# Value matmuls in four short blocks a group, output matmuls in two bunches, in a two-layer attention and experts kernel

## The chip, the cores and the metric

The kernel runs on one core of a Trainium2 chip. The metric is the device time of one execution in microseconds, median of three runs. The engines work side by side, each through its own queue in order: TensorE (PE; its weight loads are shown apart, as PEld), VectorE (DVE), ScalarE (ACT), GpSimd (POOL), and SyncE (SP), which issues the DMAs. They wait for each other by semaphores.

## The reference

There are 8 sequences of 1024 tokens of width 128, and two layers. Each layer adds attention and experts, both of the normalised input, to its input:

```python
xn = layernorm(x);  x = x + attention0(xn) + experts0(xn)
xn = layernorm(x);  x = x + attention1(xn) + experts1(xn)
```

Attention of layer 0, which the change touches, is latent attention with 8 heads. Keys and values come from a latent of 32 columns, and the output goes through W_O:

```python
scores = einsum('bhsd,bhtd->bhst', q, k) * scale      # 1024 x 1024 a head
attn = softmax(scores)
o = einsum('bhst,bhtd->bhsd', attn, v)                # v = latent @ W_UV + b
return o.transpose(...) @ W_O + b_O
```

Experts of layer 0: 8 experts, silu(x @ gate) * (x @ up) @ down, two experts a token by weight. Layer 1 has a linear attention and 8 other experts.

## The kernel before

One loop runs over the 8 sequences. The queries' heads come in two quads of four heads. A tile t is one head and one block of 128 queries; 64 tiles make 16 groups, a group g being the four heads of a quad for one block of queries (n = g % 8). Every engine has a function attention_step(w), and the steps w = 0 to 71 have, in each quad, four steps for the query projections (L1266) and 32 steps with one tile each. Which work of an older tile or group stands in step w is set by lags counted from the tile or the last tile of the group. The step of tile t is t + 4 in the first quad and t + 8 in the second.

In step w PE does the scores of tile t (L1213, 6 matmuls of 64*128 weights into two of four PSUM banks 0 to 3, after the exp of two steps before), then the 16 transposes of the probabilities of the tile of step w - 2 (L1232, into banks 4 and 5, after both copies of the tile before it), then what stands in this step of the groups. DVE takes the maximum of the scores (L863), copies the upper half of the transposed tile to probsT (L871), and in the steps 8 to 38 does one small operation of the router of the experts. ACT copies the lower half (L587) and does exp with the sum of the row (L599). probsT has room for two groups, so the copies wait for u_ready of the group two before.

The work of a group, with its lag behind the last tile's step, is this:

- lag 1: DVE takes the reciprocal of the row sums (L881)
- lags 3 and 5: PE's values(g, i), i = 0 and 1, each 16 matmuls (4 key blocks by 4 heads, 32 loads of 128*32 in the trace, L1247) that add up in the columns 0 to 127 of bank 6 + g % 2; behind i = 1 come 4 matmuls (8 loads, L1254) that spread the reciprocals in the columns 128 to 255, and u_ready
- lag 7: ACT copies these to scale_sb (L612)
- lag 8: DVE multiplies, to o_latent (L887), two slots
- lag 9: PE's output(g), one matmul (2 loads, L1261) with the quad's half of W_O, to the columns 256 to 383 of the bank
- lag 10: DVE adds them to block n of x_mid (L895); o_added lets values(g + 2, 0) start

In numbers of steps: values stand in even steps only, and output in every fourth, together with values(i = 1). After step 73 the experts of layer 0 begin (function experts, gate and up L1151, 32 units, down L1158), and PE, ACT and DVE call attention_step(74 + u) within unit u, which finishes the last groups. The gates' transposes and copy (L1129, L546) stand in step 39 and 40. The second layer does not use these steps.

The instructions of an engine run in program order, so the order of the calls is the schedule. SP loads the expert weights and the gate rows; none of its orders is written in attention_step.

Of the kernel before, what the change touches and what calls it, by code (L numbers as in the profile page):

```python
# [9 lines left out]
ALU = mybir.AluOpType  # L10
# [3 lines left out]
P = 128  # L14
BATCH = 8
SEQ = 1024
NT = SEQ // P
D = 128
BANK = 512
# [10 lines left out]
QUADS = H0 // QUAD  # L30
# [11 lines left out]
OUTPUT_LAG = 9  # L42
ADDED_LAG = 10
# [97 lines left out]
def two_layer_kernel(nc, ins, out):  # L141
    with ExitStack() as ctx:  # L142
# [26 lines left out]
        out_room = sb("out_room", [P, 2, 2, P])  # L169
        scale_sb, o_latent = out_room[:, 0, :, :], out_room[:, 1, :, :]  # L170
# [51 lines left out]
        ffn_u = [ffn_u2[:, 0, :], ffn_u2[:, 1, :], out_room[:, :, :, :].rearrange("p a b c -> p (a b c)")]  # L222
# [100 lines left out]
        o_ready = signal("o_ready", GROUPS)  # L323
        o_added = signal("o_added", GROUPS)
# [340 lines left out]
        def _(dve):  # L665
# [75 lines left out]
            for index in range(BATCH):  # L741
# [110 lines left out]
                def attention_step(w):  # L852
# [30 lines left out]
                    if g is not None:  # L883
                        if g >= 2:
                            dve.wait_ge(o_ready.sem, o_ready.at(b, g - 1))
                        dve.wait_ge(scale_ready.sem, scale_ready.at(b, g + 1))
                        nc.vector.tensor_tensor(o_latent[:, g % 2, :], ps[:, 6 + g % 2, 0:P],  # L887
                                                scale_sb[:, g % 2, :], ALU.mult).then_inc(u_scaled.sem, 1)
                    g = group_at(w, ADDED_LAG)
                    if g is not None:  # L890
                        n = g % NT
                        if g >= NT:
                            dve.wait_ge(o_added.sem, o_added.at(b, g - NT + 1))
                        dve.wait_ge(o_ready.sem, o_ready.at(b, g + 1))
                        nc.vector.tensor_tensor(x_mid[:, n, :], x_mid[:, n, :],  # L895
                                                ps[:, 6 + g % 2, 2 * P:3 * P], ALU.add
                                                ).then_inc(o_added.sem, 1)
# [46 lines left out]
                dve.wait_ge(o_added.sem, o_added.at(b, GROUPS))  # L944
# [131 lines left out]
        def _(pe):  # L1076
# [126 lines left out]
            for index in range(BATCH):  # L1203
# [33 lines left out]
                def values(g, i):  # L1237

                    if i == 0:
                        pe.wait_ge(low_copied.sem, low_copied.at(b, (g + 1) * QUAD))  # L1240
                        pe.wait_ge(high_copied.sem, high_copied.at(b, (g + 1) * QUAD))
                        if g >= 2:

                            pe.wait_ge(o_added.sem, o_added.at(b, g - 1))
                    for k in range(4 * i, 4 * i + 4):
                        for j in range(QUAD):
                            nc.tensor.matmul(ps[DC * j:DC * (j + 1), 6 + g % 2, 0:P], latent[:, k, :],  # L1247
                                             probsT[:, (g % 2) * QUAD + j, k * P:(k + 1) * P],
                                             start=(k == 0), stop=(k == NT - 1))
                    if i == 1:  # L1250
# [8 lines left out]
                def output(g):  # L1259
                    pe.wait_ge(u_scaled.sem, u_scaled.at(b, g + 1))  # L1260
                    nc.tensor.matmul(ps[:, 6 + g % 2, 2 * P:3 * P], o_latent[:, g % 2, :], w_o[:, g // NT, :],  # L1261
                                     start=True, stop=True).then_inc(o_ready.sem, 1)
# [7 lines left out]
                def attention_step(w):  # L1270
# [30 lines left out]
                    g = group_at(w, OUTPUT_LAG)  # L1301
                    if g is not None:
                        output(g)
                    for i in range(2):
                        g = group_at(w, VALUES_LAG + 2 * i)
                        if g is not None:
                            values(g, i)
# [152 lines left out]
```

## Time and profile before

| | us |
|---|---|
| median of 3 runs | 3281.0 |
| lowest and highest | 3280.36, 3284.69 |
| the profiled execution | 3290.3 |
| its span, first to last instruction | 3288.4 |
| PE busy | 2786.6 (85%) |
| DVE busy | 2251.3 (68%) |
| ACT busy | 1494.3 (45%) |
| POOL busy | 761.5 (23%) |
| mean granted TensorE clock | 0.954 |

The profile is of one execution, so its durations are summed against its own 3290.3 us. Busy shares are means over eight sequences of about 401 us, each with an attention stretch of about 180 us (steps 0 to 73) and the experts of two layers. A PE that is busy in the table may still wait inside a chain, since the ends of matmuls are modelled.

### The profile page before, as it was taken

How to read it: one execution, taken by the hardware profiler on the slowest of the kernel's cores; microseconds unless marked ns; L12 is line 12 of the kernel's file. 1: busy time of each engine (PE TensorE's matmuls, PEld its weight loads, DVE VectorE, ACT ScalarE, POOL GpSimd, SP SyncE). 2: the span in 40 equal slices, each digit the busy share in tenths (PEclk: the TensorE clock that was granted, in tenths of full speed). 3: DMA queues.
4: the chain of work that ended last, by engine and by line, in shares of the span. 5: the costliest groups of instructions: out<-in, count | busy, mean ns of one | idle time of the engine just before them, and what ended most of it. 6: DMA issues, size and time to landing. Idle time of an engine off the chain costs nothing. (4 is left out here: it accounts for less than half of the span.)

```text
span 3288.4 us, 66221 instructions
## 1 busy us (share of the span) xinstructions
PE 2786.6 (85%) x26912; PEld 1928.6 (59%) x26912; DVE 2251.3 (68%) x3638; ACT 1494.3 (45%) x2489; POOL 761.5 (23%) x566
## 2 busy tenths in 40 slices
PE   4889798897888988889888888888888888988978
PEld 2656456665556655565555655556565565655655
DVE  3874678747776478764877648775487755977558
ACT  2763237622466224662246523565135652266422
POOL 0004230052300533004320144101351023500325
PEclk7999899998999989999999999999899998999989
DMA  5002110022100221002210012000120012200112
GB/s 219 8 28 71 65 52 8 28 77 71 40 8 28 77 74 42 22 15 71 87 30 28 20 59 90 27 28 31 48 93 24 28 39 72 69 17 28 59 56 74
DMA packets 81734, 165.34 MB, mean 50 GB/s; under 512 B 8271, under 2 KB 26904, under 8 KB 80920
## 3 DMA queue, kind: packets, MB, share of 16 engines
q1 hardware_dynamic: 81432, 161.11, 14.9%
q8 instruction: 214, 3.51, 0.4%
q14 instruction: 88, 0.72, 0.1%
HBM read 147.97 MB, written 13.11 MB: 49 GB/s over the span
## 5 line engine op out<-in xcount | busy, mean ns | idle before, releaser
L498 POOL TENSOR_TENSOR probs<-ffn_gu,gate_bc 128x512 f32<-128x512 f32 x416 | 558.6, 1344 | 2268.4 <-DVE ffn_gu L925 1748.2
L1151 PE MATMUL ps<-x_parts,w_split 128*128 128x512 f32 x3072 | 941.5, 443 | 82.4 <-DVE ffn_u L964 41.7
L1151 PEld LDWEIGHTS ps<-x_parts,w_split 128*128 128x128 f32 x3072 | 570.0, 190 | 384.7 <-issue 161.3
L863 DVE TENSOR_REDUCE neg_max<-ps 128x1 f32<-128x1024 f32 x512 | 624.2, 1220 | 225.5 <-PE ps L1213 209.1
L599 ACT ACTIVATE probs<-ps,neg_max 128x1024 f32<-128x1024 f32 x512 | 571.7, 1117 | 138.4 <-DVE neg_max L863 135.0
L1232 PEld LDWEIGHTS ps<-ident,probs 64*128 64x128 f32 x8192 | 327.3, 141 | 354.9 <-issue 328.4
L1232 PE MATMUL ps<-ident,probs 64*128 64x64 f32 x8192 | 360.7, 228 | 201.3 <-DVE probsT L871 200.7
L1213 PE MATMUL ps<-keys,q_parts 64*128 64x512 f32 x3072 | 499.4, 431 | 35.2 <-ACT probs L599 21.2
L1158 PE MATMUL ps<-probs,w_down 128*128 128x512 f32 x832 | 431.1, 604 | 42.7 <-POOL probs L498 41.9
L587 ACT COPY probsT<-ps 128x512 f32<-128x512 f32 x512 | 300.5, 587 | 257.6 <-PE ps L1232 256.2
L925 DVE TENSOR_TENSOR ffn_gu<-ffn_s,ps 128x512 f32<-128x512 f32 x256 | 176.1, 688 | 332.8 <-ACT ffn_s L624 330.4
L641 ACT ACTIVATE ffn_s<-ffn_g 128x512 f32<-128x512 f32 x256 | 159.9, 631 | 459.9 <-DVE ffn_g L960 459.1
L871 DVE COPY probsT<-ps 128x512 f32<-128x512 f32 x512 | 348.8, 681 | 21.9 <-PE ps L1232 21.7
L624 ACT ACTIVATE ffn_s<-ps 128x512 f32<-128x512 f32 x256 | 153.0, 598 | 419.2 <-PE ps L1151 419.2
L1213 PEld LDWEIGHTS ps<-keys,q_parts 64*128 64x128 f32 x3072 | 256.7, 190 | 123.6 <-issue 44.8
L1247 PE MATMUL ps<-probsT,latent 128*32 128x128 f32 x8192 | 280.1, 278 | 16.1 <-DVE x_mid L895 16.1
L1247 PEld LDWEIGHTS ps<-probsT,latent 128*32 128x32 f32 x8192 | 210.0, 110 | 48.7 <-issue 26.2
L1158 PEld LDWEIGHTS ps<-probs,w_down 128*128 128x128 f32 x832 | 156.9, 191 | 108.8 <-POOL probs L498 64.5
L960 DVE TENSOR_SCALAR ffn_g<-ps,b_gate 128x512 f32<-128x512 f32 x256 | 190.8, 745 | 15.4 <-PE ps L1151 11.5
L856 DVE SCALAR_TENSOR_TENSOR q_parts<-ps,b_q,q_parts 128x1024 fp32r<-128x1024 f32 x64 | 82.1, 1283 | 119.0 <-ACT q_parts L570 119.0
L1066 DVE SCALAR_TENSOR_TENSOR ffn_gu<-ffn_u,ffn_s 128x512 f32<-128x512 f32 x176 | 134.3, 767 | 37.8 <-ACT ffn_s L641 31.8
L498 POOL TENSOR_TENSOR ffn_h<-ffn_gu,gate_bc 128x512 f32<-128x512 f32 x96 | 123.6, 1288 | 140.2 <-DVE ffn_gu L1066 95.0
(170 smaller groups left out, 2518.3 us busy)
## 6 DMA issues: line engine op xcount, KB each, us to landing
w_split<-w_parts SPq DMA_DIRECT2D x260, 256.0 KB, 2.6
gate_bc<-gate_rows SPq DMA_DIRECT2D x128, 512.0 KB, 4.2
w_parts<-q_parts SPq DMA_DIRECT2D x4, 2048.0 KB, 9.1
x_in<-in_x SPq DMA_DIRECT2D x9, 512.0 KB, 4.2
out<-x_mid SPq DMA_DIRECT2D x8, 512.0 KB, 3.2
probsT<-in_gate_up SPq DMA_DIRECT2D x1, 2048.0 KB, 8.7
gate_bc<-in_gate_up SPq DMA_DIRECT2D x1, 2048.0 KB, 13.0
w_down<-in_down SPq DMA_DIRECT2D x2, 1024.0 KB
```

The source lines that it names most:

```text
L498: nc.gpsimd.tensor_tensor(ffn_h[u % 5], ffn_gu[:, u % 3, :], gate_bc[:, e % GATE_SLOTS, c * BANK:(c + 1) * BANK], ALU.mult).then_inc(h_rea ...
L587: nc.scalar.copy(half_of(t, 0), half_turned(0)).then_inc(low_copied.sem, 1)
L599: nc.scalar.activation(probs[:, t % 3, :], banks(2 * (t % 2)), ACT.Exp, bias=neg_max[:, t % 4:t % 4 + 1], accum_out=row_sum[:, g % 2, t % ...
L863: nc.vector.tensor_reduce(neg_max[:, t % 4:t % 4 + 1], banks(2 * (t % 2)), X, ALU.max, negate=True).then_inc(max_ready.sem, 1)
L871: nc.vector.tensor_copy(half_of(t, 1), half_turned(1)).then_inc(high_copied.sem, 1)
L925: nc.vector.tensor_tensor(ffn_gu[:, u % 3, :], ffn_s[:, u % 3, :], ps[:, 2 + u % 2, :], ALU.mult).then_inc(gu_done.sem, 1)
L960: nc.vector.tensor_scalar(ffn_g[:, u % 3, :], ps[:, u % 2, :], b_gate[:, f:f + 1], LIMIT, ALU.add, ALU.min).then_inc(gate_lim.sem, 1)
L1151: mm = nc.tensor.matmul(ps[:, bank, :], w_split[:, f % 4, h, k * P:(k + 1) * P], tokens[:, half], start=(part == 0), stop=(part == 2))
L1158: nc.tensor.matmul(ps[:, 4 + c, :], w_down[l][:, f, :], ffn_h[u % 5], start=(l == 0 and f == 0), stop=(f == E * FH - 1)).then_inc(down_don ...
L1213: mm = nc.tensor.matmul(ps[:, 2 * (t % 2) + c, :], q_parts[rows, j, q, n * P:(n + 1) * P], keys[rows, k, :], start=(part == 0), stop=(part ...
L1232: mm = nc.tensor.transpose(ps[:, 4 + c, k * HQ:(k + 1) * HQ], probs[rows, t % 3, k * P:(k + 1) * P], ident[rows, rows])
L1247: nc.tensor.matmul(ps[DC * j:DC * (j + 1), 6 + g % 2, 0:P], latent[:, k, :], probsT[:, (g % 2) * QUAD + j, k * P:(k + 1) * P], start=(k == ...
```

## The change

The value matmuls of a group, before in two calls of four key blocks (lags 3 and 5), stand in four calls of two key blocks (lags 3, 4, 5, 6); the scale matmuls stay behind the last. The output matmuls of the 16 groups leave steps of their own: they run in two bunches, in steps 78 and 80 (units 4 and 6 of the first experts), each 8 matmuls for four blocks of queries, the two quads added up in PSUM, into a whole bank (6 and 7). o_latent has a slot for each group. DVE adds each bunch with one operation of 128x512 one step later, in place of 16 of 128x128. values(g, 0) waits for u_scaled of group g - 2 in place of o_added, and the multiplication L887 waits no more for o_ready.

```diff
--- before.py
+++ after.py
@@ -39,8 +39,7 @@
 VALUES_LAG = 3
 SCALES_LAG = 7
 SCALED_LAG = 8
-OUTPUT_LAG = 9
-ADDED_LAG = 10
+OUTPUT_STEPS = (STEPS + 6, STEPS + 8)
 ROUTER_STEP = 8
 ROUTER_EXP_STEPS = (18, 20)
 SPLIT_STEP = 30
@@ -166,8 +165,9 @@
         neg_max = sb("neg_max", [P, 4])
         row_sum = sb("row_sum", [P, 2, QUAD])
         inv_sum = sb("inv_sum", [P, 2, QUAD])
-        out_room = sb("out_room", [P, 2, 2, P])
-        scale_sb, o_latent = out_room[:, 0, :, :], out_room[:, 1, :, :]
+        out_room = sb("out_room", [P, BANK])
+        scale_sb = out_room[:, 0:2 * P].rearrange("p (a b) -> p a b", a=2)
+        o_latent = sb("o_latent", [P, QUADS, NT, P])
 
 
 
@@ -219,7 +219,7 @@
         ffn_s = sb("ffn_s", [P, 3, BANK])
         ffn_g, ffn_u2 = sb("ffn_g", [P, 3, BANK]), sb("ffn_u2", [P, 2, BANK])
 
-        ffn_u = [ffn_u2[:, 0, :], ffn_u2[:, 1, :], out_room[:, :, :, :].rearrange("p a b c -> p (a b c)")]
+        ffn_u = [ffn_u2[:, 0, :], ffn_u2[:, 1, :], out_room[:, :]]
         ffn_h4 = sb("ffn_h4", [P, BANK])
         ffn_gu = sb("ffn_gu", [P, 3, BANK])
 
@@ -320,8 +320,8 @@
         u_ready = signal("u_ready", GROUPS)
         scale_ready = signal("scale_ready", GROUPS)
         u_scaled = signal("u_scaled", GROUPS)
-        o_ready = signal("o_ready", GROUPS)
-        o_added = signal("o_added", GROUPS)
+        o_ready = signal("o_ready", 2)
+        o_added = signal("o_added", 2)
         x_high_ready = signal("x_high_ready", 2)
         x_low_ready = signal("x_low_ready", 2)
         raw_in = [signal(f"raw_in{l}") for l in range(2)]
@@ -881,19 +881,14 @@
                         nc.vector.reciprocal(inv_sum[:, g % 2, :], row_sum[:, g % 2, :]).then_inc(inv_ready.sem, 1)
                     g = group_at(w, SCALED_LAG)
                     if g is not None:
-                        if g >= 2:
-                            dve.wait_ge(o_ready.sem, o_ready.at(b, g - 1))
                         dve.wait_ge(scale_ready.sem, scale_ready.at(b, g + 1))
-                        nc.vector.tensor_tensor(o_latent[:, g % 2, :], ps[:, 6 + g % 2, 0:P],
+                        nc.vector.tensor_tensor(o_latent[:, g // NT, g % NT, :], ps[:, 6 + g % 2, 0:P],
                                                 scale_sb[:, g % 2, :], ALU.mult).then_inc(u_scaled.sem, 1)
-                    g = group_at(w, ADDED_LAG)
-                    if g is not None:
-                        n = g % NT
-                        if g >= NT:
-                            dve.wait_ge(o_added.sem, o_added.at(b, g - NT + 1))
-                        dve.wait_ge(o_ready.sem, o_ready.at(b, g + 1))
-                        nc.vector.tensor_tensor(x_mid[:, n, :], x_mid[:, n, :],
-                                                ps[:, 6 + g % 2, 2 * P:3 * P], ALU.add
+                    if w - 1 in OUTPUT_STEPS:
+                        c = OUTPUT_STEPS.index(w - 1)
+                        dve.wait_ge(o_ready.sem, o_ready.at(b, c + 1))
+                        nc.vector.tensor_tensor(x_mid[:, 4 * c:4 * c + 4, :], x_mid[:, 4 * c:4 * c + 4, :],
+                                                ps[:, 6 + c, :].rearrange("p (n d) -> p n d", d=D), ALU.add
                                                 ).then_inc(o_added.sem, 1)
 
                 for w in range(UNIT_STEP):
@@ -941,7 +936,7 @@
                         if k == 0:
                             dve.wait_ge(rstd_ready.sem, rstd_ready.at(b, 1))
                         norm_apply(0, x_in, (2 * k, 2 * k + 1))
-                dve.wait_ge(o_added.sem, o_added.at(b, GROUPS))
+                dve.wait_ge(o_added.sem, o_added.at(b, 2))
                 experts_add(0)
 
                 for c in range(2):
@@ -1241,13 +1236,13 @@
                         pe.wait_ge(high_copied.sem, high_copied.at(b, (g + 1) * QUAD))
                         if g >= 2:
 
-                            pe.wait_ge(o_added.sem, o_added.at(b, g - 1))
-                    for k in range(4 * i, 4 * i + 4):
+                            pe.wait_ge(u_scaled.sem, u_scaled.at(b, g - 1))
+                    for k in range(2 * i, 2 * i + 2):
                         for j in range(QUAD):
                             nc.tensor.matmul(ps[DC * j:DC * (j + 1), 6 + g % 2, 0:P], latent[:, k, :],
                                              probsT[:, (g % 2) * QUAD + j, k * P:(k + 1) * P],
                                              start=(k == 0), stop=(k == NT - 1))
-                    if i == 1:
+                    if i == NT // 2 - 1:
 
                         pe.wait_ge(inv_ready.sem, inv_ready.at(b, g + 1))
                         for j in range(QUAD):
@@ -1256,10 +1251,14 @@
                                                   start=True, stop=True)
                         mm.then_inc(u_ready.sem, 1)
 
-                def output(g):
-                    pe.wait_ge(u_scaled.sem, u_scaled.at(b, g + 1))
-                    nc.tensor.matmul(ps[:, 6 + g % 2, 2 * P:3 * P], o_latent[:, g % 2, :], w_o[:, g // NT, :],
-                                     start=True, stop=True).then_inc(o_ready.sem, 1)
+                def output(c):
+
+                    pe.wait_ge(u_scaled.sem, u_scaled.at(b, GROUPS - 1 + c))
+                    for n in range(4 * c, 4 * c + 4):
+                        for quad in range(QUADS):
+                            mm = nc.tensor.matmul(ps[:, 6 + c, (n % 4) * P:(n % 4 + 1) * P], o_latent[:, quad, n, :],
+                                                  w_o[:, quad, :], start=(quad == 0), stop=(quad == QUADS - 1))
+                    mm.then_inc(o_ready.sem, 1)
 
                 def queries(h):
                     for c in range(HALVES):
@@ -1298,11 +1297,10 @@
                         pe.wait_ge(low_copied.sem, low_copied.at(b, NT * QUAD))
                         pe.wait_ge(high_copied.sem, high_copied.at(b, NT * QUAD))
                         gates_transpose(b, 0)
-                    g = group_at(w, OUTPUT_LAG)
-                    if g is not None:
-                        output(g)
-                    for i in range(2):
-                        g = group_at(w, VALUES_LAG + 2 * i)
+                    if w in OUTPUT_STEPS:
+                        output(OUTPUT_STEPS.index(w))
+                    for i in range(NT // 2):
+                        g = group_at(w, VALUES_LAG + i)
                         if g is not None:
                             values(g, i)
 
```

## Rows read from the trace of the kernel before

**Rows 1.** The page, part 1: busy us (share of the span) xinstructions.
```profile
PE 2786.6 (85%) x26912; PEld 1928.6 (59%) x26912; DVE 2251.3 (68%) x3638; ACT 1494.3 (45%) x2489; POOL 761.5 (23%) x566
```

**Rows 2.** PE's longest wait: us in total, times, longest us.
```profile
PE ps L1232 <- DVE probsT L871: 200.7, 245, 2.3
```

**Rows 3.** Windows: us, busy (x) of PE, PEld, DVE, ACT, POOL, then granted clock.
```profile
1426.61:1436.65 10.04, 8.38 (x170) 6.49 (x166) 7.59 (x12) 7.19 (x13) 0.00 (x0) 1.00 0.01 2
...
1321.75:1331.80 10.05, 8.35 (x166) 6.45 (x162) 8.29 (x16) 7.47 (x15) 0.00 (x0) 1.00 0.01 2
...
1371.00:1389.00 18.00, 14.91 (x166) 8.01 (x164) 7.85 (x10) 6.76 (x10) 0.00 (x0) 0.91 0.01 2
```

**Rows 4.** Timeline, steps 58 to 62: start us, us, engine, line, operation [idle before].
```profile
1429.22 0.81 PEld L1247 LDWEIGHTS ps<-probsT,latent 128*32 128x32 f32 x32
...
1430.24 0.97 PE L1213 MATMUL ps<-keys,q_parts 64*128 64x512 f32 x6
...
1431.31 1.22 DVE L863 TENSOR_REDUCE neg_max<-ps 128x1 f32<-128x1024 f32 x1 [0.95 <-PE ps L1213]
...
1432.45 0.68 DVE L871 COPY probsT<-ps 128x512 f32<-128x512 f32 x1
1432.63 1.11 ACT L599 ACTIVATE probs<-ps,neg_max 128x1024 f32<-128x1024 f32 x1 [0.26 <-DVE neg_max L863]
1433.05 0.28 DVE L887 TENSOR_TENSOR out_room<-ps,out_room 128x128 f32<-128x128 f32 x1
1433.25 1.22 DVE L863 TENSOR_REDUCE neg_max<-ps 128x1 f32<-128x1024 f32 x1
...
1433.28 0.71 PE L1232 MATMUL ps<-ident,probs 64*128 64x64 f32 x16 [0.82 <-DVE probsT L871]
...
1433.92 0.30 PEld L1261 LDWEIGHTS ps<-w_o,out_room 128*128 128x128 f32 x2
...
1434.34 0.81 PEld L1247 LDWEIGHTS ps<-probsT,latent 128*32 128x32 f32 x32
...
1435.13 0.24 PEld L1254 LDWEIGHTS ps<-ident,inv_sum 128*32 128x32 f32 x8
...
1435.57 0.53 PEld L1213 LDWEIGHTS ps<-keys,q_parts 64*128 64x128 f32 x6 [0.20 <-issue]
...
1436.81 0.54 PEld L1213 LDWEIGHTS ps<-keys,q_parts 64*128 64x128 f32 x6
```

**Rows 5.** Timeline: PE at steps 16 and 36 of one sequence.
```profile
1317.79 0.53 PEld L1213 LDWEIGHTS ps<-keys,q_parts 64*128 64x128 f32 x6
...
1368.12 1.98 PE L1266 MATMUL ps<-xT,w_q 128*128 128x512 f32 x4
```

**Rows 6.** Timeline: PE at steps 45 and 73.
```profile
1395.88 0.53 PEld L1213 LDWEIGHTS ps<-keys,q_parts 64*128 64x128 f32 x6
...
1465.64 0.58 PEld L1232 LDWEIGHTS ps<-ident,probs 64*128 64x128 f32 x16 [0.20 <-issue]
```

**Rows 7.** Timeline: the border of the two quads, steps 38, 39 and 41.
```profile
1378.11 0.68 DVE L871 COPY probsT<-ps 128x512 f32<-128x512 f32 x1
...
1379.13 1.08 PE L1247 MATMUL ps<-probsT,latent 128*32 128x128 f32 x32 [2.01 <-DVE x_mid L895]
...
1380.14 3.61 PE L1266 MATMUL ps<-xT,w_q 128*128 128x512 f32 x4
...
1389.21 1.22 DVE L863 TENSOR_REDUCE neg_max<-ps 128x1 f32<-128x1024 f32 x1 [1.66 <-PE ps L1213]
```

**Rows 8.** Timeline of PE's weight loads in the experts of both layers.
```profile
1473.23 0.30 PEld L1261 LDWEIGHTS ps<-w_o,out_room 128*128 128x128 f32 x2 [0.67 <-DVE out_room L887]
...
1656.62 0.42 PEld L1158 LDWEIGHTS ps<-probs,w_down 128*128 128x128 f32 x2
...
1658.87 0.43 PEld L1158 LDWEIGHTS ps<-ffn_h,w_down 128*128 128x128 f32 x2
...
1662.91 0.43 PEld L1158 LDWEIGHTS ps<-probs,w_down 128*128 128x128 f32 x2
```

## The prediction

> **What bounds the kernel now.** I read the busy shares first [rows 1]: PE is busy 85% of the span, but in the attention it is not full, and its largest wait is that of the transposes L1232 for the DVE copy L871, 245 times and 200.7 us together [rows 2]. Then windows of four steps (one group) in either quad: 10.03 to 10.05 us each, PE not at its rate, DVE busy 7.59 us in the second quad and 8.29 us in the first, where the router's small operations stand on it, ACT 7.19 and 7.47 [rows 3]. No engine fills the 10.04 us, so a chain through several engines sets them.
>
> The timeline shows it [rows 4]. Scores of step 59 start at 1430.24; the maximum L863 starts 1.07 later (1431.31), the copy L871 1.14 after that (1432.45), the transposes of step 60 0.83 after that (1433.28): 3.04 in all. Then PE needs 0.64 for these 16 transposes, and does the work that stands behind them in step 60 before the scores of step 61 can start. So the scores of step n+2 come no earlier than 3.68 + v(n+1) after those of step n, v being PE's value, scale and output work of step n+1. The scores and transposes between, of the odd step and the scores of the even one (1435.57 to 1436.81: 1.24 for a step without group work), fit below the DVE part. There are two such chains, of odd and of even steps. Today all of v stands in even steps: 1.01 for 16 value matmuls (1429.22 to 1430.23), and 0.42 + 0.79 + 0.44 = 1.65 for output, values and scale (1433.92, 1434.34, 1435.13, 1435.57). The chain of odd scores carries both: 2 x 3.68 + 1.01 + 1.65 = 10.02, and the window says 10.03. The other chain carries nothing (7.36) and waits.
>
> **The change, part by part.** *Value matmuls in four steps.* A block of 32 loads takes 0.81 and the scores start 0.20 behind it; behind the scale matmuls there is again 0.20 [rows 4]. So a block of 16 takes, by halving the 0.81 and keeping the 0.20, 0.605. If all of it halves it is 0.505; if nothing does, 1.01. I take 0.605, as the 0.20 is the same behind a block of 32 and behind one of 8. The last block has 8 scale loads besides: 0.825. Both chains now carry two blocks: the heavier 0.605 + 0.825, so a group takes 7.36 + 1.43 = 8.79. The lighter takes 8.57 and is held by the other. Saved: 1.24 a group (1.28 in the first quad, where 1317.79 to 1368.12 are five groups of 10.07 [rows 5]).
>
> The rows show these 0.20 on the way out of a block; on the way in, behind the transposes, there is none that I can see (rival 2). A rule of the Trainium skill speaks against the change here: by TensorEngine Tiling, section Tiling Modes (Key Properties), changing the tiling mode drains the array, and two more value blocks (128*32) amid scores and transposes (64*128) make four more such changes a group. By that rule it is rival 2 that holds, 3207; by the rows the sum below.
>
> *What else must keep up at 8.79.* PE's issue work is 4 x 1.24 + 3 x 0.605 + 0.825 = 7.6. DVE's in the first quad is 8.29 less the one L895 of 0.28 = 8.0, some 8.3 with its gaps: close, but under. ACT has 7.5. Exp starts 1.32 after the maximum (1432.63) and is done before the chain gets to the scores two steps on. u_ready comes one step later (lag 6, not 5). The copies L587/L871 into the same slots of probsT, one step after it, wait for transposes that PE issues behind that block anyway; behind them on DVE stands the next maximum. So nothing is late there. The scale copy stays at lag 7.
>
> *Output matmuls and L895 leave the attention.* Each costs 0.42 in v; it is in the 1.65 already. L895, 0.20 net on DVE (as L887: 1433.05 to 1433.25), lies under the chain and is worth nothing but room. The values now wait for u_scaled, an operation that is older by two steps.
>
> *Sum for one sequence.* (a) Steps 16 to 36: 5 x 1.28 = 6.4, less about 0.64, because the chain that ends in step 36 is the even one and begins behind a value block that step 15 did not have: 5.76. (b) The border of the quads. The values of step 38 wait for L895 2.01 us, but the copy L871 that they need as well ends at 1378.79, 0.34 before they start [rows 7], so that 0.2 of it can go; with half of the values moved on, the queries at 1380.14 start 0.6 earlier. In step 40 the output and its wait no longer stand ahead of the scores of 41, whose maximum waited 1.66; the copy of the gates on ACT takes back half: 0.8. Output of step 44: 0.42. Together 1.8. (c) Steps 45 to 73, 1395.88 to 1465.64 [rows 6]: 6.5 groups x 1.24 = 8.06, and 0.65 at the end, where step 72 has no output and half the values: 8.7. (d) First experts, where PE is the limit: leave 1.01 (step 74), 1.65 and a wait of 0.67 (step 76, [rows 8]), 0.42 (step 80) = 3.75. Come 3 x 0.605 + 0.825 = 2.64 for group 15, and two bunches of 8 matmuls = 16 loads each. Nearest row: the 16 loads of the same shape of the projection stretch one unit from 2.25 (1656.62 to 1658.87) to 4.04 (to 1662.91) [rows 8], so 1.79 each, 3.58. Net +2.47. The two additions of four blocks (128x512) lie on DVE in units where it waits for PE's 2.25 us units.
> Sum: 5.76 + 1.8 + 8.7 - 2.47 = 13.8 us, eight times 110. No DMA and no SP or POOL instruction is moved.
> The profiled execution took 3290.3 (span 3288.4), 9.3 above the median of 3281.0. 3290.3 - 110 = 3180; the median scaled alike 3281 - 110 = 3171.
>
> **The clock.** At the border of the quads, behind the wait of 2.01 us, the queries take 3.61 [rows 7] where the same four took 1.98 [rows 5]: that stretch ran at 1.2 GHz, the one before at 2.4, and the window around it has a mean granted clock of 0.91 [rows 3]. The wait shrinks to about 1; if the clock then stays up, 1.6 us more are won, 13 in eight sequences. I leave it as it is in the sum, and put it in the range.
>
> **Rivals.**
> 1. *All small costs fall away:* blocks of 0.505 (0.2 more a group, 11.5 groups: 2.3), clock up at the border (1.6), the lighter chain sets the last step (1.0): 13.8 + 4.9 = 18.7 a sequence, 3131. For it: nothing but the shortness of the blocks; against: the 0.20 stands behind every one. Chance 0.13.
> 2. *A short block pays on its way in too.* With another 0.20 for each of the two blocks of a chain the period is 9.19, 11.5 x 0.40 = 4.6 us of gain go in a sequence: 9.2 left, 3207. For it: a block amid transposes and scores is a change of shape on both sides. Against: in rows 4 the values' loads start 0.12 behind the output's and close behind the transposes. Chance 0.10.
> 3. *Short blocks cost as much as long ones, or DVE becomes the bound in the first quad.* With 1.01 a block: 7.36 + 1.01 + 1.23 = 9.60, so only 0.43 a group; 11.5 x 0.81 = 9.3 less gain, 0.8 more in the experts: 3.7 a sequence, 3252. With DVE bound at 9.4 in the first quad: 5 x 0.6 = 3 less, 3195; both in part: 3215 to 3250. Chance 0.10.
> 4. *Nothing of the period is won:* another wait takes it, say the maximum held behind DVE's own queue at 10.03. Left are 1.8 + 0.65 - 2.47, that is 0: 3281. The DVE sum of 7.6 in the second quad speaks against it. Chance 0.03.
> 5. *Slower:* u_ready a step later does hold the copies of the group after next, and with them maximum, exp and scores behind them. If each group lost a whole step of 2.2, 25.3 would go in a sequence: 11.5 slower, 3373. It decides from 1.2 us a group on. Against it: the copy waits for transposes issued behind the block. Chance 0.04.
> Forecast as summed, with small deviations either way (3145 to 3200): 0.60.
>
> **How the numbers follow.** A measurement tells 0.2% (6.6 us) from no change. The forecast and rivals 1 to 3 are faster: 0.93; rival 4 is the same, 0.03; rival 5 slower, 0.04. Range: 3135 takes in most of rival 1, 3215 rival 2 and the DVE bound; outside are the rest of rival 3, rivals 4 and 5 and the end of 1, less than 0.2.
>
> **What the profile after should show.** Value loads in blocks of 16, each followed by 0.20; four-step windows of 8.8 us (8.6 to 9.0) in both quads, nearly even steps of 2.2; L1232's wait for L871 far below 200 us but not gone, in pieces of 0.3; DVE's share up to 70% or more; the output line with 256 loads as before, in bunches of 16 that stretch two units by 1.8. Wrong would be: windows of 9.2 or 9.6 (the block cost), windows of 10 (another wait), L871 waiting with PE's L1254 as releaser (rival 5), or long stretches at 1.2 GHz inside the quads.

## The result and the profile after

The changed kernel takes 3170.25 us (median of 4 runs, 3162.18 to 3171.23), the kernel before on the same chip 3282.85 (4 runs, 3280.36 to 3288.09). The ratio is 0.965, 95% interval 0.9629 to 0.967: 3.5% faster, where 3171 was forecast. The profiled execution took 3170.15, its span is 3168.1, against 3288.4 before.

The page of the changed kernel, part 1:

```profile
PE 2811.7 (89%) x26912; PEld 1902.6 (60%) x26912; DVE 2245.2 (71%) x3526; ACT 1494.5 (47%) x2489; POOL 760.9 (24%) x566
```

PE has as many instructions as before, and its share has gone from 85% to 89% [rows 1]: the span is 120 us shorter because PE waits less. The view of PE's waits in the changed kernel says which; its columns are us in total, times, and the longest:

```profile
PE ps L1227 <- DVE probsT L871: 62.1, 103, 2.0
```

The transposes (L1227 now, L1232 before) wait 62.1 us for the copy L871 in place of 200.7, and 103 times in place of 245 [rows 2]; that is 0.6 a time, where the prediction looked for pieces of 0.3. Two windows of one group (four steps) each, columns as in [rows 3]:

```profile
1376.50:1385.27 8.77, 8.54 (x165) 6.18 (x162) 7.57 (x11) 7.23 (x14) 0.00 (x0) 1.00 0.02 5
1385.27:1394.02 8.75, 8.51 (x164) 6.16 (x161) 7.57 (x11) 7.23 (x14) 0.00 (x0) 1.00 0.01 2
```

A group takes 8.75, and took 10.04. DVE's and ACT's work in it is what it was; it is packed closer. The timeline of the second of these groups (start, length, engine, operation, idle before):

```profile
1385.27 0.53 PEld L1208 LDWEIGHTS ps<-keys,q_parts 64*128 64x128 f32 x6 [0.20 <-issue]
...
1386.67 0.38 PEld L1242 LDWEIGHTS ps<-probsT,latent 128*32 128x32 f32 x16
...
1387.24 0.53 PEld L1208 LDWEIGHTS ps<-keys,q_parts 64*128 64x128 f32 x6 [0.20 <-issue]
...
1388.32 0.71 PE L1227 MATMUL ps<-ident,probs 64*128 64x64 f32 x16
...
1388.96 0.38 PEld L1242 LDWEIGHTS ps<-probsT,latent 128*32 128x32 f32 x16
...
1389.54 0.53 PEld L1208 LDWEIGHTS ps<-keys,q_parts 64*128 64x128 f32 x6 [0.20 <-issue]
...
1391.50 0.53 PEld L1208 LDWEIGHTS ps<-keys,q_parts 64*128 64x128 f32 x6 [0.20 <-issue]
...
1393.22 0.38 PEld L1242 LDWEIGHTS ps<-probsT,latent 128*32 128x32 f32 x16
...
1393.58 0.24 PEld L1249 LDWEIGHTS ps<-ident,inv_sum 128*32 128x32 f32 x8
...
1394.02 0.53 PEld L1208 LDWEIGHTS ps<-keys,q_parts 64*128 64x128 f32 x6 [0.20 <-issue]
```

Every step holds a block of 16 value loads now, and the scores of the next step start 0.58 after the block does (1388.96 to 1389.54: 0.38 and 0.20); with the scale loads it is 0.80 (1393.22 to 1394.02). One group of the heavier chain: 1385.27 to 1389.54 is 4.27 (3.68 + 0.58 = 4.26), and 1389.54 to 1394.02 is 4.48 = 3.68 + 0.80. Sum 8.75.

Where the time of one sequence goes, from starts in the two traces (means over the eight sequences; the quad stretches between the 12th and 32nd, the 32nd and 38th, and the 38th and last maximum L863; the experts from the 1st to the 32nd multiplication L920):

| stretch | before | after | difference |
|---|---|---|---|
| first maximum to step 15 | 26.2 | 25.7 | -0.5 |
| steps 15 to 35 (first quad) | 50.3 | 45.0 | -5.3 |
| steps 35 to 45 (border of the quads) | 29.1 | 26.6 | -2.5 |
| steps 45 to 71 (second quad) | 64.5 | 56.5 | -8.1 |
| to the first L920 of the experts | 9.2 | 7.7 | -1.5 |
| first experts, units 0 to 31 | 70.0 | 73.2 | +3.2 |
| rest of the experts, into the next sequence | 153.1 | 152.6 | -0.5 |

The sum is -15.3 a sequence, 122 in eight (the last row counts seven times), and the spans differ by 120.3.

The border: PE's operations there in the changed kernel, from the timeline.

```profile
1326.11 0.64 PE L1242 MATMUL ps<-probsT,latent 128*32 128x128 f32 x16 [0.97 <-issue]
...
1326.69 1.98 PE L1265 MATMUL ps<-xT,w_q 128*128 128x512 f32 x4
```

The wait ahead of the values is 0.97 in place of 2.01, and the queries behind it take 1.98 in place of 3.61 [rows 7]: the granted clock stayed at 2.4 GHz where it had gone to 1.2.

The first experts of the changed kernel, PE's loads:

```profile
1403.97 0.38 PEld L1242 LDWEIGHTS ps<-probsT,latent 128*32 128x32 f32 x16 [0.36 <-issue]
1404.55 1.22 PEld L1146 LDWEIGHTS ps<-x_parts,w_split 128*128 128x128 f32 x6 [0.20 <-issue]
...
1412.51 0.42 PEld L1153 LDWEIGHTS ps<-probs,w_down 128*128 128x128 f32 x2
...
1413.60 1.75 PEld L1259 LDWEIGHTS ps<-w_o,o_latent 128*128 128x128 f32 x15 [0.24 <-issue]
...
1416.55 0.43 PEld L1153 LDWEIGHTS ps<-probs,w_down 128*128 128x128 f32 x2
...
1418.81 0.42 PEld L1153 LDWEIGHTS ps<-probs,w_down 128*128 128x128 f32 x2
```

A unit with a bunch of output matmuls takes 4.04 (1412.51 to 1416.55), the next without one 2.26: 1.78 for a bunch, 1.79 was forecast. The value blocks among the gate matmuls are another matter. The weight loads stand idle for 0.36 ahead of such a block and for 0.20 behind it. What a block costs in all shows in the distance from one unit's multiplication L920 on DVE to the next one's. In the changed kernel, a unit with a short block:

```profile
1404.71 0.69 DVE L920 TENSOR_TENSOR ffn_gu<-ffn_s,ps 128x512 f32<-128x512 f32 x1 [2.51 <-ACT ffn_s L624]
1406.88 0.69 DVE L920 TENSOR_TENSOR ffn_gu<-ffn_s,ps 128x512 f32<-128x512 f32 x1 [1.48 <-ACT ffn_s L624]
```

In g1_last_two, an experiment below that has long blocks there, a unit with a long block, one without a block, and one with a long block and the scale:

```profile
1405.26 0.69 DVE L920 TENSOR_TENSOR ffn_gu<-ffn_s,ps 128x512 f32<-128x512 f32 x1 [2.51 <-ACT ffn_s L624]
1407.86 0.69 DVE L920 TENSOR_TENSOR ffn_gu<-ffn_s,ps 128x512 f32<-128x512 f32 x1 [1.91 <-ACT ffn_s L624]
1409.22 0.69 DVE L920 TENSOR_TENSOR ffn_gu<-ffn_s,ps 128x512 f32<-128x512 f32 x1 [0.47 <-ACT ffn_s L624]
1412.04 0.69 DVE L920 TENSOR_TENSOR ffn_gu<-ffn_s,ps 128x512 f32<-128x512 f32 x1 [2.13 <-ACT ffn_s L624]
```

That is 2.17 with a short block, 2.60 with a long one, 1.36 without, 2.82 with a long one and the scale. A short block adds about 0.80 there and a long one 1.24, where the prediction had 0.605 and 1.01.

### The profile page after: what moved, and what is told of

It is laid out like the page before. It is cut to its first block and busy times, and to the rows that moved or that the text cites. A ratio compares the mean times of both kernels' runs of the same rounds, so it can differ in the third digit from the quotient of the medians.

```text
span 3168.1 us, 65933 instructions
## 1 busy us (share of the span) xinstructions
PE 2811.7 (89%) x26912; PEld 1902.6 (60%) x26912; DVE 2245.2 (71%) x3526; ACT 1494.5 (47%) x2489; POOL 760.9 (24%) x566
## 3 DMA queue, kind: packets, MB, share of 16 engines
q1 hardware_dynamic: 81432, 161.11, 15.3%
## 5 line engine op out<-in xcount | busy, mean ns | idle before, releaser
L863 DVE TENSOR_REDUCE neg_max<-ps 128x1 f32<-128x1024 f32 x512 | 624.5, 1221 | 113.8 <-PE ps L1208 78.8
L1227 PEld LDWEIGHTS ps<-ident,probs 64*128 64x128 f32 x8192 | 323.9, 141 | 246.4 <-issue 228.1
L1227 PE MATMUL ps<-ident,probs 64*128 64x64 f32 x8192 | 362.0, 228 | 81.8 <-DVE probsT L871 62.1
L920 DVE TENSOR_TENSOR ffn_gu<-ffn_s,ps 128x512 f32<-128x512 f32 x256 | 175.9, 687 | 350.1 <-ACT ffn_s L624 347.6
L871 DVE COPY probsT<-ps 128x512 f32<-128x512 f32 x512 | 348.2, 680 | 13.2 <-PE ps L1227 13.2
L1242 PE MATMUL ps<-probsT,latent 128*32 128x128 f32 x8192 | 331.9, 280 | 7.8 <-issue 7.8
L1242 PEld LDWEIGHTS ps<-probsT,latent 128*32 128x32 f32 x8192 | 193.7, 109 | 64.1 <-issue 33.6
```

What stands on the lines that cost most here:

```text
L863: nc.vector.tensor_reduce(neg_max[:, t % 4:t % 4 + 1], banks(2 * (t % 2)), X, ALU.max, negate=True).then_inc(max_ready.sem, 1)
L871: nc.vector.tensor_copy(half_of(t, 1), half_turned(1)).then_inc(high_copied.sem, 1)
L920: nc.vector.tensor_tensor(ffn_gu[:, u % 3, :], ffn_s[:, u % 3, :], ps[:, 2 + u % 2, :], ALU.mult).then_inc(gu_done.sem, 1)
L1227: mm = nc.tensor.transpose(ps[:, 4 + c, k * HQ:(k + 1) * HQ], probs[rows, t % 3, k * P:(k + 1) * P], ident[rows, rows])
```

## The experiments

The theory is that of the prediction: two chains of steps, scores n+2 = scores n + 3.68 + v(n+1), so what matters is how PE's group work is shared between odd and even steps. Rivals: that the bunches (less work in the quads, fewer waits) bring the gain, or that PE's work in a group as a whole counts, wherever it stands. In the first four, each part alone and two other splits of the values.

### e1_values4: the values in four steps, the outputs as before

```diff
 (kernel before)
-                    for k in range(4 * i, 4 * i + 4):
+                    for k in range(2 * i, 2 * i + 2):
...
-                    if i == 1:
+                    if i == NT // 2 - 1:
...
-                    for i in range(2):
-                        g = group_at(w, VALUES_LAG + 2 * i)
+                    for i in range(NT // 2):
+                        g = group_at(w, VALUES_LAG + i)
```

> The kernel before with the value matmuls in four steps (lags 3 to 6), outputs as before. Theory of the two chains (scores of step n+2 not before 3.68 us + group work of step n+1): even steps carry 0.60 + 0.60 + 0.42 of output, a group takes 8.98 us, eight sequences give some 100 us, and the clock at the border of the quads stays up as in the changed kernel: 3165 to 3185 us. Rival (the gain comes from taking outputs and their additions off the queues): at most half of the 113 us of the whole change, 3225 or more.

Measured: 3172.85 (4 runs, 3166.88 to 3183.30), ratio 0.9672 (0.9649 to 0.9696). Steps 15 to 35 take 45.7, steps 45 to 71 57.7, the first experts 70.1. So the split of the values brings all of the gain. A group takes 8.95 in the second quad, and the sum of the two chains is 8.98. The bunches bring 0.7 and 1.2 more in the quads and 0.8 at their border, and pay 3.1 in the experts: nothing net that can be told at the interval. The profiled executions lie 13 us apart (spans 3181.4 and 3168.1), and that is not the bunches' doing either: 14 us of it are the last row of the table, 154.6 for 152.6, whose code is the same in both.

### e2_bunches: the changed kernel with the values in lags 3 and 5 again

```diff
 (changed kernel)
-                    for k in range(2 * i, 2 * i + 2):
+                    for k in range(4 * i, 4 * i + 4):
...
-                    if i == NT // 2 - 1:
+                    if i == 1:
...
-                    for i in range(NT // 2):
-                        g = group_at(w, VALUES_LAG + i)
+                    for i in range(2):
+                        g = group_at(w, VALUES_LAG + 2 * i)
```

> The changed kernel with the value matmuls in two steps as before (lags 3 and 5), so the bunches alone. Two chains: both blocks in even steps, 7.36 + 1.01 + 1.23 = 9.60 us a group, less 2 us of bunches in the experts: 3235 to 3265 us. Rival (outputs are the cost): 3225 or less.

Measured: 3264.11 (3262.80 to 3265.33), ratio 0.9947 (0.9932 to 0.9962). Starts of the scores in its timeline (PE):

```profile
1420.91 0.96 PE L1208 MATMUL ps<-keys,q_parts 64*128 64x512 f32 x6
1422.17 0.94 PE L1208 MATMUL ps<-keys,q_parts 64*128 64x512 f32 x6
...
1430.52 0.96 PE L1208 MATMUL ps<-keys,q_parts 64*128 64x512 f32 x6
```

A group takes 9.61 (1420.91 to 1430.52): 2 x 3.68 + 1.01 + 1.23 = 9.60. Without the output matmul of 0.42 in the heavy chain a group is 0.42 shorter, and that is all that the bunches do for it.

### e3_lags34: two blocks of 16 matmuls in neighbouring steps (lags 3 and 4)

```diff
 (changed kernel)
-                    for k in range(2 * i, 2 * i + 2):
+                    for k in range(4 * i, 4 * i + 4):
...
-                    if i == NT // 2 - 1:
+                    if i == 1:
...
-                    for i in range(NT // 2):
+                    for i in range(2):
                         g = group_at(w, VALUES_LAG + i)
```

> The changed kernel with the values of a group in two blocks of 16 matmuls, but in neighbouring steps (lags 3 and 4), so one in an even and one in an odd step, and none in the other two. Two chains: each carries one block, the heavier 7.36 + 1.23 = 8.59 us a group, and the experts have two short blocks less: 3145 to 3165 us, below the changed kernel's 3170. Rival (what helps is that every step carries the same, PE having no empty steps): worse than the changed kernel by a good part of the way back, 3200 to 3250.

Measured: 3264.18 (3263.02 to 3268.09), ratio 0.9951 (0.9932 to 0.9969). This missed: each chain carries one block, and yet a group takes 9.10. One group in its timeline:

```profile
1420.22 0.96 PE L1208 MATMUL ps<-keys,q_parts 64*128 64x512 f32 x6
...
1422.84 0.96 PE L1208 MATMUL ps<-keys,q_parts 64*128 64x512 f32 x6
...
1423.91 1.22 DVE L863 TENSOR_REDUCE neg_max<-ps 128x1 f32<-128x1024 f32 x1 [0.60 <-ACT probs L599]
...
1425.05 0.68 DVE L871 COPY probsT<-ps 128x512 f32<-128x512 f32 x1
...
1425.73 1.19 DVE L863 TENSOR_REDUCE neg_max<-ps 128x1 f32<-128x1024 f32 x1
...
1426.84 0.68 DVE L871 COPY probsT<-ps 128x512 f32<-128x512 f32 x1
...
1427.67 0.71 PE L1227 MATMUL ps<-ident,probs 64*128 64x64 f32 x16 [0.20 <-DVE probsT L871]
...
1428.31 0.81 PEld L1242 LDWEIGHTS ps<-probsT,latent 128*32 128x32 f32 x32
...
1429.32 0.54 PEld L1208 LDWEIGHTS ps<-keys,q_parts 64*128 64x128 f32 x6 [0.20 <-issue]
```

The trace shows a third chain, which passes from one step to the next on DVE. Two heavy steps stand in a row: the scores behind the second start 2.62 after those behind the first (1420.22, 1422.84). From there 1.07 to the maximum, 1.14 to its copy L871, and the next maximum follows that copy on DVE at once (0.68); 1.11 to its copy, 0.83 to the transposes, 0.64 to the value block, 1.01 to the scores: 2.62 + 1.07 + 1.14 + 0.68 + 1.11 + 0.83 + 0.64 + 1.01 = 9.10. In the changed kernel the same chain is 1.97 (1385.27 to 1387.24) + 5.47 + 0.58 = 8.02, below the 8.75 of the heavier parity chain, so there it doesn't show. The first quad bears the chain out: there a small router operation stands on DVE between that copy and the next maximum, the maximum starts 0.92 behind the copy and not 0.68, and a group takes 9.37 in place of 9.10. Even parity is not enough; the work has to be even from step to step.

The quads (47.6 in seven of eight sequences, and 59.3, against 45.0 and 56.5) make 5.4 a sequence, 43 of its 94 us. The rest lies mostly outside them: 28.5 for 26.6 at their border, 8.5 for 7.7 behind the second, 155.6 for 152.6 in the last stretch, with a mean granted clock of 0.945 in place of 0.961 over the span.

### e4_1313: the four steps with 1, 3, 1 and 3 key blocks

```diff
 (changed kernel)
-                    for k in range(2 * i, 2 * i + 2):
+                    for k in ((0,), (1, 2, 3), (4,), (5, 6, 7))[i]:
```

> The changed kernel with one, three, one, three key blocks in the four steps. Same work, same number of blocks. Two chains: odd steps carry 0.78 + 1.00, a group takes 9.14 us in place of 8.75: 3198 to 3215 us. Rival (only the total of PE and the number of blocks count): 3165 to 3175.

Measured: 3210.84 (3209.74 to 3217.74), ratio 0.9789 (0.9772 to 0.9807); steps 15 to 35 take 46.7, steps 45 to 71 58.7. Two maxima of its second quad, one group apart (DVE):

```profile
1388.79 1.23 DVE L863 TENSOR_REDUCE neg_max<-ps 128x1 f32<-128x1024 f32 x1
...
1397.98 1.22 DVE L863 TENSOR_REDUCE neg_max<-ps 128x1 f32<-128x1024 f32 x1
```

A group takes 9.19, where the sum of the chain is 9.14. As many matmuls and as many blocks as in the changed kernel, only uneven over the parities: of its gain of 112.6 us, 40.6 are lost. In the profiled executions, which lie 48 us apart, 32 of them stand in the quads and 13 in the last stretch, whose code is the same.

### e5_odd and e6_even: 16 more matmuls a group on the light chain, or on the heavy one

Both add to the kernel before 16 value matmuls a group whose weights are zeros, so that they add nothing to the sums; only the lag at which they stand differs.

```diff
 (kernel before; e6_even has 3 in place of 4)
...
+            nc.vector.memset(zeros[:, :], 0.0)
...
+                    g = group_at(w, 4)
+                    if g is not None and g < GROUPS - 1:
+                        for k in range(4):
+                            for j in range(QUAD):
+                                nc.tensor.matmul(ps[DC * j:DC * (j + 1), 6 + g % 2, 0:P], zeros[:, :],
+                                                 probsT[:, (g % 2) * QUAD + j, k * P:(k + 1) * P],
+                                                 start=False, stop=False)
```

> The kernel before with 16 more matmuls a group (of the form of the values, weights of zeros, so they add nothing) in an odd step (lag 4), where PE has no group work. They take 0.81 + 0.20 us, 15 times a sequence: 121 us of PE in all. Two chains: the chain that they load has 1.66 us of room, so only the block at the border of the quads shows: 0 to +12 us, 3281 to 3295. Rival (PE's total counts): +100 to +120 us, 3380 to 3400.

> The kernel before with the same 16 matmuls more a group in an even step (lag 3), directly behind the values there. Two chains: the full 0.81 us each time, 12 to 15 times a sequence: +78 to +97 us, 3360 to 3380. Rival (PE's total counts): the same as in the odd step.

Measured: e5_odd 3284.39 (10 runs, 3280.95 to 3294.15) beside 3283.44 of the kernel before, ratio 1.0005 (0.9996 to 1.0015). e6_even 3377.85 (3366.48 to 3390.01), ratio 1.0295 (1.0271 to 1.0319). The same 1920 matmuls (16 in 15 groups of 8 sequences) change nothing that can be told on one chain and cost 94 us on the other. A group of the second quad, in e5_odd (PE's loads) and in e6_even (DVE):

```profile
1430.76 0.53 PEld L1215 LDWEIGHTS ps<-keys,q_parts 64*128 64x128 f32 x6 [0.20 <-issue]
...
1440.89 0.53 PEld L1215 LDWEIGHTS ps<-keys,q_parts 64*128 64x128 f32 x6 [0.20 <-issue]
```

```profile
1458.28 1.23 DVE L865 TENSOR_REDUCE neg_max<-ps 128x1 f32<-128x1024 f32 x1 [1.84 <-PE ps L1215]
...
1469.17 1.23 DVE L865 TENSOR_REDUCE neg_max<-ps 128x1 f32<-128x1024 f32 x1 [1.82 <-PE ps L1215]
```

It takes 10.13 and 10.89, and 10.03 in the kernel before: 0.10 on the light chain, 0.86 on the heavy one. The light chain had 2.66 of room (10.02 - 7.36), so the block of 1.01 fits in with 1.65 to spare. This rules out that PE's work in a group as a whole sets the time. That e5_odd comes out at no change at all is partly luck. Its quads take 0.9 a sequence more, and its border 1.0 more where both ran at the full clock (28.5 for 27.5), some 15 us in all; the granted clock gave that back (mean 0.963 over its span, 0.954 in the profiled execution before).

### g1_last_two and g2_values4_last_two: the last group's values in two blocks

What the changed kernel loses in the experts is in part the short blocks of group 15. Here that group alone has two blocks of 16 matmuls; g1_last_two is the changed kernel with it, g2_values4_last_two is e1_values4 with it.

```diff
 (changed kernel)
                 def values(g, i):
+                    if g == GROUPS - 1:
+                        if i % 2:
+                            return
+                        blocks = range(4 * (i // 2), 4 * (i // 2) + 4)
+                    else:
+                        blocks = range(2 * i, 2 * i + 2)
...
-                    for k in range(2 * i, 2 * i + 2):
+                    for k in blocks:
...
-                    if i == NT // 2 - 1:
+                    if blocks[-1] == NT - 1:
```

> The changed kernel, but the values of the last group (15), which run within the first experts, in two blocks of four key blocks (lags 3 and 5) in place of four. If a value block among the experts' matmuls costs 0.36 us on its way in and 0.20 on its way out, two blocks fewer give 1.1 us a sequence: the stretch of the first experts falls from 73.2 to 72.1 us, the time by 9 us to 3161. Rival (PE's gaps there are waits for other engines): no change, 3170.

> Value matmuls in four steps with the outputs as in the kernel before (the first experiment), and the last group in two blocks. The same 1.1 us a sequence below that experiment's 3172.9: 3164. If bunches of outputs are worth something once the values are spread, it is slower than the one before it in this list by that.

Measured: g1_last_two 3181.43 (3178.78 to 3182.40), ratio 0.9685 (0.9664 to 0.9706); g2_values4_last_two 3177.09 (3171.97 to 3179.94), ratio 0.9673 (0.9653 to 0.9692). Both missed. In g1_last_two the first experts are shorter by 0.7 a sequence (72.5 for 73.2), where 1.1 was expected: the four short blocks add 3 x 0.80 + 1.02 = 3.4 and the two long ones 1.24 + 1.46 = 2.7, so not all of the 0.36 ahead of a block is the block's own cost. In g2_values4_last_two they are shorter by only 0.2, since the output matmul of step 76 waits 0.67 for L887 again, as in the kernel before. The time did not follow: in g1_last_two the last stretch, whose code is the same, takes 155.6 to 156.3 in six of seven sequences, where it took 151.5 to 153.6. One case, at the start of the second layer's experts, is the window 1500 to 1515 of g1_last_two (after the busy times stands the mean granted clock):

```profile
1500.00:1515.00 15.00, 10.79 (x33) 7.11 (x32) 8.44 (x17) 0.00 (x0) 0.00 (x0) 0.84 0.00 0
```

and the same window of the changed kernel:

```profile
1500.00:1515.00 15.00, 9.95 (x42) 6.54 (x40) 10.26 (x21) 0.80 (x1) 0.00 (x0) 1.00 0.00 0
```

In the window before (1476 to 1500) both have a mean granted clock of 0.72. PE's gate matmuls behind the same wait, in g1_last_two:

```profile
1506.92 2.65 PE L1146 MATMUL ps<-x_parts,w_split 128*128 128x512 f32 x6 [2.08 <-DVE ffn_g L955]
```

and the changed kernel:

```profile
1506.63 1.62 PE L1146 MATMUL ps<-x_parts,w_split 128*128 128x512 f32 x6 [2.08 <-DVE ffn_g L955]
```

The same wait, the same six matmuls, 0.29 apart in time: in g1_last_two they take 2.65, at a mean granted clock of 0.55, that is mostly at 1.2 GHz; in the changed kernel 1.62, at 2.4 GHz.

### g3_dve_small: one more 128x64 DVE operation in each step of the second quad

The first quad gained less than five groups of 1.28, and I put that down to the router's small operations on DVE. The changed kernel, with one such operation a step in the second quad as well (and from step 40, at the end of the border), on tiles that nobody reads then:

```diff
 (changed kernel)
...
+                        if 40 <= w < 72:
+                            link(nc.vector.tensor_tensor(r_e[:, :, :], r_d[:, :, :], r_d[:, :, :], ALU.add))
```

> The changed kernel with one more small DVE operation (128x64, with its wait, as the router's) behind each copy L871 in the steps of the second quad. If it is these operations that make a group of the first quad 9.0 us and not 8.7, the second quad becomes the same: steps 45 to 71 take 58.5 in place of 56.4 us, and the time rises by 15 to 20 us to 3185 to 3190. Rival (they lie in DVE's idle time, and the first quad is slower for another reason): 3170 to 3174.

Measured: 3182.52 (3181.84 to 3183.13), ratio 0.9689 (0.9665 to 0.9714). The time is near the forecast of the theory and the stretch is not. Steps 45 to 71 take 56.7, 0.3 more: 0.04 a group, so small operations are not it. Of the five groups of the first quad in the changed kernel, four take 8.77 to 8.79 in most sequences and the last 9.77. DVE's timeline there, in the changed kernel:

```profile
1304.34 1.23 DVE L863 TENSOR_REDUCE neg_max<-ps 128x1 f32<-128x1024 f32 x1
...
1306.54 1.21 DVE L849 TENSOR_TENSOR x_parts<-xT,x_parts 128x1024 fp32r<-128x1024 f32 x1
1307.67 1.22 DVE L863 TENSOR_REDUCE neg_max<-ps 128x1 f32<-128x1024 f32 x1
```

One long operation, L849 for the experts' x_parts, stands on DVE between two maxima, and that step takes 3.33 (1304.34 to 1307.67). It takes 3.33 before as well, but there the heavy steps took 3.14 anyway, and its group 10.08. So the 12 us in the time say nothing for the theory: 2 are in the second quad, the rest at the borders (27.1 for 26.6, where these operations stand too, and up to 156.2 in the last stretch).

### h1_pad4 and h2_pad10: more work ahead of the border

If the last stretch of g1_last_two is longer only by where in time the clock's stretches at 1.2 GHz fall, then more work ahead of it can make the kernel faster. g1_last_two, with 4 or 10 repeated matmuls of 128x512 in unit 20 of the first experts (into a bank that is started anew behind them):

```diff
 (g1_last_two; h2_pad10 has 10 in place of 4)
+                    if l == 0 and u == 20:
+                        for i in range(4):
+                            nc.tensor.matmul(ps[:, u % 2, :], w_split[:, f % 4, 0, 0:P], x_high[:, half],
+                                             start=True, stop=True)
```

> The kernel with the last group in two blocks (3181.4 us), with four repeated matmuls of 128x512, about 0.9 us, in unit 20 of the first experts of each sequence. In that kernel 155.9 us pass from the last unit of the first experts to the first maximum of the next sequence, in the changed kernel 151.7 to 153.6, since there PE stays at 2.4 GHz in the first gate and up matmuls of the second layer. Theory: whether it does depends on when in time the border of the layers comes, not on the work; then more work can make the kernel faster or leave it alone: 3155 to 3182 us. Rival (the slow clock belongs to the shorter value blocks' change): 8 x 0.9 us more, 3188 to 3190.

> The same with ten repeated matmuls, about 2.2 us a sequence. Theory: the part after the border shortens by up to 4 us in some or all sequences: 3165 to 3185 us. Rival (work counts as such): 8 x 2.2 us more than 3181.4, 3198 to 3200.

Measured: h1_pad4 3177.85 (3174.0 to 3180.3), ratio 0.967 (0.9653 to 0.9688); h2_pad10 3191.68 (3189.41 to 3194.01), ratio 0.9716 (0.9702 to 0.9731). With four more matmuls the first experts take 73.4, 0.9 more than in g1_last_two, 7 us in all; the last stretch takes 153.6 to 153.9 in five of seven sequences, 2 less, and the median is 3.6 us lower, which the two intervals do not tell apart; what can be told is that the 7 us more of work do not show. With ten, the experts take 74.8, 18 us more in all, and the time is 10.3 longer: outside what I expected of the theory (3165 to 3185) and below what the rival needs (3198 to 3200). That the time of the last stretch shifts with work ahead of it is shown by the stretches of one profiled execution each; a rule by which it could be foretold is not.

## Why the prediction was right, and where its terms were off

*The bound* [rows 2, 4]: right. e5_odd and e6_even show the two chains directly, and the length of a group follows the sum of the heavier chain in four kernels: 8.75 for 8.79 here, 8.95 for 8.98 (e1_values4), 9.61 for 9.60 (e2_bunches), 9.19 for 9.14 (e4_1313). Incomplete in one place: the third chain, over DVE, that e3_lags34 brought out; it doesn't bind in either kernel.

*The block.* 0.605 forecast, 0.58 measured; with the scale 0.825 and 0.80. Period 8.79 and 8.75. In the quads the 0.20 stands on the way out alone, as the rows said.

*(a), steps 16 to 36:* 5.76 forecast, 5.3 measured from step 15 to 35, and 5.4 over the prediction's own stretch. Four groups gained 1.28 each; the fifth, in which L849 sets a step, gained 0.3 (10.08 to 9.77). The 0.64 that was taken off for the first step did not show: L849 took 1.0 instead, which the prediction did not have.

*(b), the border of the quads:* 1.8 forecast, 2.5 measured, but of two parts. In the one sequence of before in which the clock stayed up, this stretch took 27.5; against it the change wins 1.0. The other 1.5 is the clock: the 1.6 that the prediction named and left out of its sum. e1_values4, with the clock up, has 27.4 there: the split values win 0.1 of the 1.0, where the prediction had 0.6 for them, and the outputs the rest.

*(c), steps 45 to 73:* 8.7 forecast; 8.1 to step 71, and 0.7 in the stretch behind it in the sequences of before that ran at the full clock (8.3 or 8.4, and now 7.6 or 7.7). The remaining 0.8 of that row comes from three sequences of before with 10.5 to 11.0, part of them at 1.2 GHz.

*(d), the first experts:* +2.47 forecast, +3.2 measured. The bunches are right at 1.78. The value block was mis-sized there: the prediction took its cost amid scores and transposes, and among 128x512 matmuls it costs more, a short one 0.80 and not 0.605, a long one 1.24 and not 1.01. So the four that come add 3.4, where 2.64 was reckoned. What leaves is 3.6, not 3.75: 1.24 in unit 0, 2.20 in unit 2 with the output and its wait, and 0.20, not 0.42, for the output matmul of step 80 (that unit took 2.46, its neighbours 2.26). With the bunches' 3.56 that gives +3.3, and the sequences of before that the clock left alone have +3.3.

The Trainium skill (TensorEngine Tiling, section Tiling Modes, Key Properties) says that a change of tiling mode drains the array. The traces agree in the idle time of 0.20 of the weight loads behind every value block. Ahead of a block they show 0.36 behind 128x512 matmuls, part of it the block's own cost as above, and nothing behind the transposes in the quads. That the draining is the reason of these times is not shown.

*The sum.* Without the clock the change is worth 5.3 + 1.0 + 8.1 + 0.7 - 3.2 and 0.4 in the first row of the table (sequences with the same share of slow clock: 25.6 to 25.9 before, 25.3 to 25.5 after), a row that the prediction did not have: 12.3 a sequence, 98 us in eight, where the prediction had 13.8 and 110. The clock gave about 3 a sequence in the profiled executions (15.3 - 12.3): 1.5 at the border of the quads, 0.8 behind the second quad, 0.5 in the last row and the rest in the first. So the forecast was right in its mechanism and, in the part that it summed, within 12%. That it came within 1 us of the median is luck: the part that it summed was 12 us too large, and the clock, which it left out, gave some 15 of the 112.6 between the medians.

*The rivals.* 1 (all small costs fall away) did not come: the 0.20 stands. 2 (a short block pays more) held in the experts alone, with 0.2 a block. 3: the block of 1.01 did not come, and DVE bound one step of 20 in the first quad (L849), not all of it. 4 and 5 would have needed groups of 10 or more, and the longest takes 9.8.

What stays open is what decides at each border at which point the granted clock goes down and up again. Neither g2_values4_last_two nor g3_dve_small was followed by a run that holds the border fixed.

## What to carry to other kernels

Where no engine is full, follow one tile through the engines to the same point again and see how many steps lie between: if two, the odd and the even steps can be chains of their own, and then work costs little on the light one (e5_odd, e6_even: the same matmuls cost 0.10 a group on it and 0.86 on the heavy one). Spread work evenly over every step, not only over the chains, as other chains link neighbouring steps (e3_lags34). Judge changes below 1% by stretches of the trace and not by the time alone: a stretch with the same code moved by 2 to 4 us a sequence though nothing in it had been changed.

## What the runs showed of the hardware

The granted clock at a recurring idle place is not a fixed price. The last stretch of a sequence, whose code is the same in all these kernels, took 151.5 to 156.4 us. In the changed kernel it took 151.5 to 153.6 at a mean granted clock of 0.93 or 0.92, in g1_last_two 155.6 to 156.3 at 0.91 in six of seven sequences; the matmuls behind a wait ran at 1.2 or at 2.4 GHz (2.65 or 1.62 for six of 128x512). The seven such stretches of an execution add up to 1068 us in the one and 1089 in the other, and it can go against the work: g1_last_two has less work than the changed kernel and took 11 us more (ratios 0.9685 and 0.965, whose intervals just overlap), and the 7 us more of work in h1_pad4 did not show. The same program moves with it as well: nine runs of the kernel before took 3273.1 us at a mean granted clock of 0.960 to 3293.35 at 0.954.

The cost of a block of weight loads of another shape depends on its place. Sixteen loads of 128*32 cost 0.58 amid scores and transposes and about 0.80 amid 128x512 matmuls; 32 loads cost 1.01 and 1.24.
